# Each expert's add to the output issued as two DMAs of 64 rows

## What is computed

```python
x = L0_attn_X
x = x + 0.5 * ffn(_layernorm(x, axis=-1), ...)
x = x + attn(_layernorm(x, axis=-1), ...)
x = x + 0.5 * ffn(_layernorm(x, axis=-1), ...)
```

```python
T, E, K, F, CAP = 4096, 32, 4, 176, 128
w_topk, sel = jax.lax.top_k(probs, K)
...
g = jnp.einsum('ech,ehf->ecf', buf, w_gate)      # buf: up to CAP tokens of each expert
u = jnp.einsum('ech,ehf->ecf', buf, w_up)
y = jnp.einsum('ecf,efh->ech', jax.nn.silu(g) * u, w_down)
...
out = jnp.zeros((T, Hq), x.dtype).at[tok].add(gath * wv[:, None])
sh = jax.nn.silu(x @ sw_gate) * (x @ sw_up) @ sw_down
sh = jax.nn.sigmoid(x @ w_shared_gate) * sh
out = out + sh
```

## Time and profile before

| | |
|---|---|
| runs | 939.25, 943.64, 944.14 us; median 943.64 |
| profiled execution, span of its instructions | 937.5 us |
| the median of the runs, above this span | 6.1 us |
| TensorE busy | 910.2 us, 97% |
| VectorE, ScalarE, GpSimd busy | 74%, 57%, 55% |
| first ffn's experts, first to last add | 155.0 to 297.7 us |
| second ffn's experts, first to last add | 766.5 to 908.6 us |
| granted TensorE clock, mean | 0.999 |

### The profile page before, as it was taken

How to read it: one execution, slowest core, us unless ns; L and a number is a source line. 1 busy time by engine, 2 the same in 40 slices (tenths; PEclk the granted TensorE clock), 3 DMA queues, 4 the chain that set the end, 5 groups by cost and what they waited for, 6 DMA issues and landing times.

```text
span 937.5 us, 18000 instructions
## 1 busy us (share of the span) xinstructions
PE 910.2 (97%) x6118; PEld 685.5 (73%) x6118; DVE 696.1 (74%) x1704; ACT 531.8 (57%) x794; POOL 511.3 (55%) x537
## 2 busy tenths in 40 slices
PE   7999999999999999999999999989999999999997
PEld 6878887777778856666666666558788877777786
DVE  6998787554444889989998999988887875544435
ACT  6666743132233478878887888876667431322322
POOL 6343305555652588887888788934432045655530
PEclk9999999999999999999999999999999999999999
DMA  8143228777774510010001002004432187777725
GB/s 260 49 137 107 74 86 214 178 178 182 181 191 92 179 46 24 23 42 26 23 23 45 22 12 79 24 12 131 142 99 73 56 232 173 183 178 183 173 38 178
DMA packets 95512, 101.89 MB, mean 109 GB/s; under 512 B 18768, under 2 KB 86736, under 8 KB 95440
## 3 DMA queue, kind: packets, MB, share of 16 engines
q1 hardware_dynamic: 83152, 83.17, 28.7%
q0 software_dynamic: 12288, 17.83, 11.2%
HBM read 65.44 MB, written 35.54 MB: 108 GB/s over the span
## 4 chain that ended last, share of the span: by engine, by line
PE 67%; DVE 18%; issue 6%; ACT 5%; POOL 3%; DMA 0%; DVEq 0%; POOLq 0%; SPq 0%; ACTq 0%
PE zT L1048 8%; PE gu L1068 7%; PE gu L90 7%; PE gu L92 6%; PE gu L91 6%; PE pj_at L90 3%; PE down L90 3%; PE down L92 3%; PE down L91 3%; PE pv_at L1766 3%; PE pj_at L92 3%; PE pj_at L91 3%; PE zT L1057 2%; PE scores_at L1750 2%; DVE turned_at L2008 2%
## 5 line engine op out<-in xcount | busy, mean ns | idle before, releaser
L90 PE MATMUL gu<-x_hi,gu_hi 128*128 128x512 f32 x264 | 120.7, 457 | 0.8 <-DVE act_gu L1351 0.7
L820 POOL DMA_INDIRECT rows<-z_rows,slots x64 | 69.0, 1078 | 67.7 <-DVE slots L1342 49.1
L1868 ACT ACTIVATE capped_at<-scores_at 128x2048 f32<-128x2048 f32 x64 | 93.1, 1455 | 20.5 <-PE scores_at L1750 20.2
L92 PE MATMUL gu<-x_lo,gu_hi 128*128 128x512 f32 x264 | 103.9, 394 | 0.0
L91 PE MATMUL gu<-x_hi,gu_lo 128*128 128x512 f32 x264 | 103.6, 392 | 0.0
L1128 ACT CAST a_hi<-act_gu 128x512 fp32r<-128x512 f32 x96 | 59.2, 617 | 75.9 <-DVE act_gu L1351 63.1
L1876 ACT ACTIVATE probs_at<-capped_at 128x2048 f32<-128x2048 f32 x64 | 95.1, 1486 | 2.5
L90 PE MATMUL down<-down_hi,a_hi 128*128 128x256 f32 x300 | 93.9, 313 | 0.6 <-DVE a_lo L1361 0.4
L1230 ACT ACTIVATE y<-gu,rows 128x256 f32<-128x256 f32 x64 | 30.3, 474 | 109.7 <-PE gu L1068 94.6
L1945 POOL TENSOR_SCALAR_AFFINE_SELECT probs_at<-probs_at 128x1024 f32<-128x1024 f32 x64 | 85.6, 1342 | 9.6 <-ACT probs_at L1876 8.9
L1048 PE MATMUL zT<-w_gu,xT 128*128 128x352 f32 x256 | 86.3, 460 | 0.0
(11 more groups left out here) (262 smaller groups left out, 2602.5 us busy)
## 6 DMA issues: line engine op xcount, KB each, us to landing
w_gu<-in_w_gate SPq DMA_DIRECT2D x64, 176.0 KB, 2.6
w_gu<-in_w_up SPq DMA_DIRECT2D x64, 176.0 KB, 3.2
w_down<-in_w_down SPq DMA_DIRECT2D x64, 176.0 KB
z_rows<-z SPq DMA_DIRECT2D x16, 512.0 KB, 3.8
acc<-base SPq DMA_DIRECT2D x10, 512.0 KB, 3.2
out<-base SPq DMA_DIRECT2D x10, 512.0 KB, 3.2
xn_at<-acc SPq DMA_DIRECT2D x16, 256.0 KB, 2.7
x<-xn_at SPq DMA_DIRECT2D x16, 256.0 KB, 2.1
```

The lines of the kernel that those rows point to most:

```text
L90: nc.tensor.matmul(out, w_hi, x_hi, start=first, stop=False)
L92: return nc.tensor.matmul(out, w_hi, x_lo, start=False, stop=last)
L820: pool.indirect_dma_start(out=gathered_rows[:, n, :], out_offset=None, in_=m.z_rows, in_offset=bass.IndirectOffsetOnAxis(ap=slots[:, e:e + ...
L1868: nc.scalar.activation(capped[:, u % 2, :, 0:n], scores[:, :, 0:n], ACT.Tanh, scale=QK_SCALE / SOFTCAP).then_inc(capped_ready, 1)
```

## The change

Each add is issued as two indirect DMAs of 64 rows: partitions 0 to 63 of y by `slots`, partitions 64 to 127 by a second list, `slots_upper`, which holds the token numbers of the upper 64 partitions in partitions 0 to 63. The second DMA follows the first without a wait. Both count on `added`, which now counts 32 per expert. `add(e)` still waits for all halves of the experts before it. VectorE makes the second list by one more instruction for each group of four experts, and it is that one which reports the lists.

```diff
+        ADDED = 2 * 16
...
+        slots_upper = sb("slots_upper", [P // 2, E], I32)
...
-        added = sem("added", 16 * E)
+        added = sem("added", ADDED * E)
...
-            reached(sp, added, 16 * E)
+            reached(sp, added, ADDED * E)
...
             def add(e):
-                at_least(pool, added, 16 * e)
+                at_least(pool, added, ADDED * e)
                 reached(pool, y_scaled, e + 1)
-                pool.indirect_dma_start(
-                    out=acc, out_offset=bass.IndirectOffsetOnAxis(ap=slots[:, e:e + 1], axis=0),
-                    in_=y[:, e % HELD_Y, :], in_offset=None, compute_op=ALU.add,
-                    bounds_check=last_row, oob_is_err=True).then_inc(added, 16)
+                for half, rows_at in enumerate((slots, slots_upper)):
+                    pool.indirect_dma_start(
+                        out=acc, out_offset=bass.IndirectOffsetOnAxis(ap=rows_at[0:P // 2, e:e + 1], axis=0),
+                        in_=y[half * P // 2:(half + 1) * P // 2, e % HELD_Y, :], in_offset=None, compute_op=ALU.add,
+                        bounds_check=last_row, oob_is_err=True).then_inc(added, 16)
...
-                at_least(act, added, 16 * (e - HELD_Y + 1))
+                at_least(act, added, ADDED * (e - HELD_Y + 1))
...
                 dve.scalar_tensor_tensor(out=slots[:, r * 4:(r + 1) * 4], in0=token[:, s], scalar=-float(P),
-                                         in1=local[:, s], op0=ALU.add, op1=ALU.add).then_inc(lists_ready, 1)
+                                         in1=local[:, s], op0=ALU.add, op1=ALU.add)
+                dve.scalar_tensor_tensor(out=slots_upper[:, r * 4:(r + 1) * 4], in0=token[P // 2:P, s],
+                                         scalar=-float(P), in1=local[P // 2:P, s], op0=ALU.add,
+                                         op1=ALU.add).then_inc(lists_ready, 1)
```

## The result

The changed kernel takes 1000.16 us (median of four runs, 994.06 to 1001.99) against 941.44 us for the kernel before: a ratio of 1.0623, with a 95% interval of 1.0592 to 1.0654, so 59 us slower. The forecast was 951.3, at most 982, that is 7.7 us slower and at most 38.

A forecast was written before the change was run, and what follows sets the result against it. TensorE, 4.56 us an expert, was taken as the bound, the adds' chain hidden by 0.11; a step of 4.86 us would add 7.3 (stage 1) + 0.2 (stage 2) + 0.2 (list) = +7.7 us: 951.3 us, range 942 to 982.

The forecast's parts named there:

- What bounds the kernel: Expert stretches: TensorE paces at 4.56 us an expert; the GpSimd chain of adds, 4.45 us a step, is hidden.
- The issue of 64 rows: GpSimd issue of each half add: estimated 1.05 us, between 0.80 (all per row) and 1.59 (all fixed).
- the 0.54 us between an add's and a gather's issue: GpSimd issues of 1.59 and 1.05 us: difference taken as the price of 128 rows, leaving 0.51 us fixed.
- The rest of the sum: Step 4.86 us, last landing 8.6 us later per stage; +7.3 in stage 1, +0.2 in stage 2, +0.2 for the list.
- The saved data time: First half's rows move while the second is issued: 0.41 us less after the last issue of each add.
- spare times: Delay absorbed after the last add: 1.3 us before stage 1's attention statistics, 8.4 us before stage 2's reload is wanted.
- The gathers: Gather for six experts on, queued behind the add's wait: wanted 27 us later, so 9 us of lag cost nothing.
- the limit of lag: Among the experts: 13 us of lag before ScalarE, waiting for a free y buffer, blocks and TensorE stops behind it.
- The list: Second list on VectorE: first gather of each stage 0.16 us later, +0.2 us in all, between 0 and 0.3.
- B: Rival: add issue mostly fixed (1.2 us and more) or no data time saved; 977 to 1020 us; chance 0.27.
- its loss among the experts: Rival B at 1020 us: lag passes 13 us, ScalarE's wait for a free y stops TensorE among the experts.
- C: Rival: the two halves of an add move one after the other, +1.2 us landing; 1002 us; chance 0.05.

The follow-up runs named there:

- the work put ahead of and behind the add: Kernel before plus an unused GpSimd power on 128x5 values: ahead of each add 1001.57 us against 939.16; behind it 944.89 us, ratio 1.0062.
- The plain scatter: Kernel before with the addition taken out of the indirect DMA, so it overwrites the output's rows: 938.93 us in one run against 938.96.
- a lone half: Changed kernel without the adds of the upper 64 tokens, so only the first half is issued: 942.20 us, ratio 1.0023 to the kernel before.

## Why the prediction was wrong

**What bounds the kernel** was read rightly: TensorE at 4.56 us an expert, the adds hidden beside it by 0.11 us. That a larger step would fall behind y, and that the last landing of each stage decides, is shown by the work put ahead of and behind the add.

**The issue of 64 rows is the step that failed.** The prediction took 1.05 us between bounds of 0.80 and 1.59; it is 1.40 to 1.43. The two issues and their gap thus cost +1.54 us a step, where the prediction had +0.82. It had read the 0.54 us between an add's and a gather's issue as the price of 128 rows. The plain scatter shows that they do belong to the addition, but the three sizes show 2.6 ns a row and 1.25 us fixed, and two sizes of a gather, at the same place, 0.9 ns a row and 0.93 us fixed. So of the 0.54 us, 1.25 - 0.93 = 0.32 are fixed too; the fixed part that the prediction put at 0.51 is 1.25. One difference between two operations at one size can't tell what of it is fixed; only a second size can, and the trace had none. The nearest bound, all fixed, was closer than the estimate between.

The page of the Trainium skill that I had set beside it, "GPSIMD Engine Reference", section 4 (When to use GPSIMD), tells of a pair of cores for reads and writes; nothing in these runs speaks against that, but it didn't bear the price that I hung on the split of the work.

**The rest of the sum holds as a whole.** With 1.43 + 1.40 + 0.30 - 1.59 - 0.41 = +1.13 us the prediction's own steps give 5.58 us (5.64 and 5.45 measured), a last landing 31 x 1.02 - 1.1 + 1.1 = 31.6 us later, of which 30.3 and 23.2 pass: +53.5 us, and about 57 with what the list costs. The spans differ by 54.8, the medians by 58.7. By stage it meets less well: 32.3 us passed at the first joint, and 18.7 between the first y of stage 2 (800.7, 35.6 late) and the first user of the reload (54.3 late). Some of the nearness of the total is luck. The saved data time of 0.41 us is 0.4 (2.6 - 2.2 above). Of the spare times, 1.3 us was 1.7 and 8.4 was 9.4.

**The gathers.** That 27 us lie between a gather's place in the list and its use was wrong, and the limit of lag with it: TensorE waited 13.4 us for gathered rows in stage 1. `turn_rows(e + 6)` runs ahead of `gate_up_expert(e + 5)`, and so about four experts after the y of e, not six; the add and the gather's own landing come off that. In the kernel before, the gather for the seventh expert and the turning of its rows:

```profile
768.38 1.06 POOL L820 DMA_INDIRECT rows<-z_rows,slots  x1 [0.31 <-issue]
783.61 0.41 PEld L1039 LDWEIGHTS zT<-ident,rows 128*128 128x128 f32 x2
```

15.2 us lie between, 3.7 of them a gather's landing in this stage, at the median. Lag beyond some 11.5 us is thus passed to TensorE, and from there the y come at the pace of the adds: the distance from y to add grows to 15.4 us by the 13th expert of stage 1 and ends at 14.7. More of this wait cost nothing, as the kernel with fewer buffers shows; it put part of TensorE's idle time among the experts.

**The list** was taken at 0.2 us and costs 3.4. I had counted one instruction ahead of the first gather where three stand ahead of the first expert, and had not thought of the tiles that a new one moves.

**The rivals.** B was the right one, mostly fixed issue. Its figure for the end of the range, 1020 us, was too high because the issue stops at 1.40, and its loss among the experts came by another wait: ScalarE waited only 2.3 us for a free y in stage 1, TensorE 13.4 for gathered rows. C gave 1002 us, 58 more than before where 59 was measured, by luck, for its cause isn't there: the upper half lands 3.5 us after its own start, a lone half 3.6. The Trainium skill, "DMA: Bandwidth & Descriptors", section Rules for kernel authors, advises against two transfers to disjoint partition halves because they serialize on the same engines. The advice holds here. Its reason isn't what this trace shows: the halves are paid for at their issue, on GpSimd. **The chances** gave slower 0.60, but the range ended at 982 with 0.27 on B, whose upper part I left out as unlikely without a row that said so.

## What to carry to other kernels

Count an indirect DMA by its instructions, not by its rows: halving an add from 128 to 64 rows took 10 to 12% off its issue. Look at where an issue stands: between two landings of a serial chain it counts in full once the chain is the longest, beside a landing it costs little, as long as the engine's own work stays under the pace of the bound. And where a hidden chain is within a few per cent of the bound, work out what one instruction more makes of it over all its turns, with its price at both ends of the bounds.

## What the runs showed of the hardware that I had not expected

- The issue of an indirect DMA with addition took 1.59, 1.40 and 1.30 us for 128, 64 and 32 rows (1.59 as a first part, the others as later ones), without addition 1.04 for 128; a gather took 1.05 and 0.95 to 0.99 us for 128 and 64.
- A computation on GpSimd put behind an add is recorded as started half a microsecond before that add's issue is over. Its record is also half a microsecond longer, 1.72 us instead of the 1.20 ahead of the add, so no run shows that the two really work at the same time. The kernel with the work behind, in order of time:

```profile
207.56 1.58 POOL L829 DMA_INDIRECT acc<-y,slots  x1 [0.63 <-DMA acc<-y,slots]
208.66 1.72 POOL L834 TENSOR_TENSOR filler<-ones_f,neg_half 128x5 f32<-128x5 f32 x1
210.56 1.09 POOL L821 DMA_INDIRECT rows<-z_rows,slots  x1 [0.18 <-issue]
```

- A tile of 128 bytes that nothing uses made the kernel 0.08% slower, with an interval that ends at nothing, and its first experts 0.9 us late.
